# A gated cross-attention and mixture-of-experts block on one core: TensorE's order inside a step of the attention loop

## The reference

```python
h   = layernorm(x)                                  # x: 32 x 64 x 512, 2048 rows in all
q   = rmsnorm(h @ Wq.T  -> 32 heads x 128) * q_norm_w
k   = rmsnorm(ctx @ Wk.T -> 8 heads x 128) * k_norm_w
v   = ctx @ Wv.T                                    # 8 heads x 128, each serves 4 query heads
p   = softmax(q @ k.T / sqrt(128) + mask)           # 64 x 64 for each of 32 batches and 32 heads
x   = x + tanh(g_xattn) * ((p @ v) @ Wo.T)
h2  = layernorm(x)
out = x + tanh(g_ffn) * (shared_ffn(h2) + top-2-of-16 mixture of experts (h2))
```

## Time and profile before

| what | value |
|---|---|
| time, median of 3 executions | 1516.77 us (1516.59 to 1519.57) |
| time of the profiled execution | 1513.25 us |
| its span | 1511.2 us |
| TensorE matmuls busy | 1435.7 us, 95% of the span |
| VectorE busy | 852.8 us, 56% |
| ScalarE busy | 508.4 us, 34% |
| GpSimd busy | 353.0 us, 23% |
| chain that ended last | 90% of it on TensorE |

### The profile page before, as it was taken

One profiled execution on the slowest core, in us unless ns is written; L12 is line 12 of the kernel. 1 busy time (PEld: TensorE's weight loads), 2 busy tenths in 40 slices (PEclk: granted clock), 3 DMA queues, 4 the chain that ended last, 5 costly groups with the idle time before them and its releaser, 6 DMA issues.

```text
span 1511.2 us, 31305 instructions
## 1 busy us (share of the span) xinstructions
PE 1435.7 (95%) x10606; PEld 1222.2 (81%) x10607; DVE 852.8 (56%) x1839; ACT 508.4 (34%) x1130; POOL 353.0 (23%) x407
## 2 busy tenths in 40 slices
PE   6999999999999999999999999999997999999980
PEld 5888888888888888888888888888885888777760
DVE  5444446656566566665665666656879532233335
ACT  4333343333333333333333333333334411222210
POOL 1222232211212212112122121221212071233335
PEclk9999999999999999999999999999998999999995
DMA  6534331111111111111111111111224083355548
GB/s 217 160 118 132 121 112 39 35 39 32 42 35 35 38 38 35 38 31 42 35 35 38 36 37 39 32 38 54 69 69 154 21 177 103 130 165 165 167 156 261
DMA packets 92737, 125.39 MB, mean 83 GB/s; under 512 B 9009, under 2 KB 58208, under 8 KB 92192
## 3 DMA queue, kind: packets, MB, share of 16 engines
q1 hardware_dynamic: 85360, 104.21, 22.3%
q0 software_dynamic: 7344, 20.73, 4.8%
HBM read 87.39 MB, written 37.53 MB: 83 GB/s over the span
## 4 chain that ended last, share of the span: by engine, by line
PE 90%; DMA 3%; DVE 3%; issue 1%; POOL 1%; ACT 0%; SPq 0%; POOLq 0%; DVEq 0%
PE ps L499 23%; PE ps L501 22%; PE ps L500 22%; PE ps L774 5%; PE ps L566 5%; PE ps L606 4%; PE ps L790 3%; PE ps L575 2%; PE ps L592 2%; DMA y<-ybuf,sli 1%; PE ps L769 1%; POOL y L479 1%; DMA acc<-in_wv 1%; PE ps L547 1%; DMA wgu<-in_w_gu 1%
## 5 line engine op out<-in xcount | busy, mean ns | idle before, releaser
L422 POOL TENSOR_TENSOR qr<-qv,mhalf 128x8 f32<-128x8 f32 x64 | 105.1, 1642 | 733.8 <-DVE qv L1123 733.8
L499 PE MATMUL ps<-hT,w0h 128*128 (+2 forms) x640 | 199.1, 311 | 0.9 <-DVE w0l L1056 0.9
L501 PE MATMUL ps<-hT,w0h 128*128 (+2 forms) x640 | 196.2, 306 | 0.0
L500 PE MATMUL ps<-hT,w0l 128*128 (+2 forms) x640 | 196.0, 306 | 0.0
L1108 DVE TENSOR_TENSOR acc<-ps,acc 128x512 f32 (+1 forms) x129 | 88.7, 688 | 146.6 <-PE ps L501 146.6
L932 ACT CAST ah<-ps 128x256 fp32r<-128x256 f32 x256 | 83.5, 384 | 256.7 <-PE ps L501 253.9
L1114 DVE TENSOR_TENSOR al<-ps,ah 128x256 fp32r<-128x256 f32 x256 | 96.2, 418 | 99.4 <-ACT ah L932 99.2
L499 PE MATMUL ps<-hT,w1h 128*128 (+1 forms) x512 | 147.6, 288 | 0.0
L500 PE MATMUL ps<-hT,w1l 128*128 (+1 forms) x512 | 145.1, 283 | 0.0
L501 PE MATMUL ps<-hT,w1h 128*128 (+1 forms) x512 | 145.0, 283 | 0.0
L499 PEld LDWEIGHTS ps<-hT,w0h 128*128 128x128 f32 x640 | 123.2, 192 | 7.8 <-DVE w0l L1056 1.1
(11 more groups left out here) (211 smaller groups left out, 3179.1 us busy)
## 6 DMA issues: line engine op xcount, KB each, us to landing
wraw<-in_w_att SPq DMA_DIRECT2D x64, 256.0 KB, 2.6
ybuf<-ye SPq DMA_DIRECT2D x47, 256.0 KB, 2.0
vbuf<-vo SPq DMA_DIRECT2D x16, 512.0 KB, 3.3
kbuf<-ko SPq DMA_DIRECT2D x16, 512.0 KB, 3.8
kt<-kbuf SPq DMA_DIRECT2D x64, 128.0 KB, 2.0
vt<-vbuf SPq DMA_DIRECT2D x64, 128.0 KB, 2.0
wgu<-in_w_gu SPq DMA_DIRECT2D x4, 2048.0 KB, 12.8
craw<-in_ctxT SPq DMA_DIRECT2D x9, 512.0 KB, 4.9
```

What stands on the lines that cost most here:

```text
L422: pool.tensor_tensor(qr[:], qv[:], mhalf[:, 0:8], ALU.pow).then_inc(q_rt, 1)
L499: pe.matmul(dst, l_hi, r_lo, start=first, stop=False)
L500: pe.matmul(dst, l_lo, r_hi, start=False, stop=False)
L501: return pe.matmul(dst, l_hi, r_hi, start=False, stop=last)
```

## The change

TensorE's order in a step becomes Q 1 to 4, transposes, scores, sums, both output projections of step i - 1, and then probabilities times v. The transposed probabilities go to PS[0] instead of PS[2] and PS[3]. TensorE waits ahead of them until ScalarE has squared the new Q there. The scores wait for the two copies of Q one by one. ScalarE's and VectorE's queues are reordered to match: ScalarE splits its weight slice and makes the exponentials ahead of `a_hi_tile`, and VectorE runs `a_rest` at the end of its step. Before the loop, GpSimd clears all of `ah` and `al` instead of half of each. As both projections lag by a step, step 0 projects two cleared tiles instead of one, and four tiles instead of three are projected behind the loop: tiles 0 and 1 of step 62 around the last transposes, tiles 0 and 1 of step 63 at the end. The diff, with little context:

```diff
@@ -415,7 +415,7 @@
             for t in (ah, al):
-                pool.memset(t[:, 1].rearrange("p h b s -> p (h b s)").bitcast(F32), 0.0).then_inc(acc_zero, 1)
+                pool.memset(t[:].rearrange("p a h b s -> p (a h b s)").bitcast(F32), 0.0).then_inc(acc_zero, 1)
@@ -558,9 +558,9 @@
             def scores(j):
-                pe.wait_ge(q_copy, 2 * j + 2)
                 pe.wait_ge(kt_in, 16 * j + 16)
                 for hp in range(2):
+                    pe.wait_ge(q_copy, 2 * j + 1 + hp)
                     for b in range(CB):
@@ -589,7 +589,8 @@
                     src = pb[:, CB * (m // 2) + 2 * (m % 2):CB * (m // 2) + 2 * (m % 2) + 2, :]
-                    mm = pe.transpose(PS[2 + m % 2][:, m // 2 * P:(m // 2 + 1) * P], src.rearrange("p b s -> p (b s)"), ident[:])
+                    c0 = m % 2 * HG * S + m // 2 * P
+                    mm = pe.transpose(PS[0][:, c0:c0 + P], src.rearrange("p b s -> p (b s)"), ident[:])
                 mm.then_inc(pT_done, 1)
@@ -608,7 +609,13 @@
-            def step(i, chunk_q, w_q, w_o, w_before, q_ready, o_ready):
+            def project_tile(i, bp, w_o):
+                pe.wait_ge(a_hi, 4 * i + 6 + 2 * bp)
+                pe.wait_ge(a_lo, 4 * i + 6 + 2 * bp)
+                pe.wait_ge(acc_done, 2 * i + 3 + bp)
+                project_out(bp, w_o, (0, 1, 2, 3))
+
+            def step(i, chunk_q, w_q, w_o, q_ready, o_ready):
@@ -618,18 +625,15 @@
                 q_head(1, 0, chunk_q, w_q)
+                q_head(1, 1, chunk_q, w_q).then_inc(q_done, 1)
+                pe.wait_ge(q_sq, 2 * i + 3)
                 transpose_probs(i)
-                q_head(1, 1, chunk_q, w_q).then_inc(q_done, 1)
-                probs_v(i)
                 scores(i + 1)
                 q_sums(i + 1)
-                pe.wait_ge(acc_done, 2 * i + 1)
-                project_out(1, w_before, (0, 1, 2, 3))
                 pe.wait_ge(w_lo, o_ready)
-                pe.wait_ge(a_hi, 4 * i + 6)
-                pe.wait_ge(a_lo, 4 * i + 6)
-                pe.wait_ge(acc_done, 2 * i + 2)
-                project_out(0, w_o, (0, 1, 2, 3))
+                for bp in range(2):
+                    project_tile(i - 1, bp, w_o)
+                probs_v(i)
@@ -639,11 +643,11 @@
             def group(i0, p, last=False):
-                step(i0, 1, W[p], W[p], W[1 - p], None, i0 + 8)
+                step(i0, 1, W[p], W[1 - p], None, i0 + 8)
                 with pe.Fori(0, NC - 2) as t:
-                    step(i0 + 1 + t, t + 2, W[p], W[p], W[p], None, i0 + 8)
+                    step(i0 + 1 + t, t + 2, W[p], W[p], None, i0 + 8)
                 if not last:
-                    step(i0 + NC - 1, 0, W[1 - p], W[p], W[p], i0 + 12, i0 + 8)
+                    step(i0 + NC - 1, 0, W[1 - p], W[p], i0 + 12, i0 + 8)
@@ -651,20 +655,12 @@
-            pe.wait_ge(acc_done, 2 * STEPS - 1)
-            pe.wait_ge(a_hi, 4 * STEPS)
-            pe.wait_ge(a_lo, 4 * STEPS)
-            project_out(1, W[1], (0, 1, 2, 3))
+            project_tile(STEPS - 2, 0, W[1])
             transpose_probs(STEPS - 1)
+            project_tile(STEPS - 2, 1, W[1])
             probs_v(STEPS - 1)
-            pe.wait_ge(a_hi, 4 * STEPS + 2)
-            pe.wait_ge(a_lo, 4 * STEPS + 2)
-            pe.wait_ge(acc_done, 2 * STEPS)
-            project_out(0, W[1], (0, 1, 2, 3))
-            pe.wait_ge(a_hi, 4 * STEPS + 4)
-            pe.wait_ge(a_lo, 4 * STEPS + 4)
-            pe.wait_ge(acc_done, 2 * STEPS + 1)
-            project_out(1, W[1], (0, 1, 2, 3))
+            project_tile(STEPS - 1, 0, W[1])
+            project_tile(STEPS - 1, 1, W[1])
@@ -686,7 +682,7 @@
                 if c == 2:
-                    pe.wait_ge(acc_done, 2 * STEPS + 3)
+                    pe.wait_ge(acc_done, 2 * STEPS + 4)
                 for k in range(KD):
@@ -921,12 +917,10 @@
                 for bp in range(2):
-                    act.copy(pt[0][:, bp, :], PS[2 + bp][:, 0:HG * S]).then_inc(pT_hi, 1)
+                    act.copy(pt[0][:, bp, :], PS[0][:, bp * HG * S:(bp + 1) * HG * S]).then_inc(pT_hi, 1)
...
             def a_hi_tile(i, bp):
-                if bp == 1:
-                    act.wait_ge(o_done, 2 * i + 1)
-                    act.wait_ge(a_lo, 4 * i + 6)
+                act.wait_ge(o_done, 2 * i + 1 + bp)
                 for b2 in range(2):
@@ -940,13 +934,13 @@
                 squares(0, i + 1)
-                probs_hi(i)
                 q_out(1, i + 1)
                 squares(1, i + 1)
+                probs_hi(i)
+                split_slice(i, w, sl)
+                exps(i + 1)
                 a_hi_tile(i, 0)
                 a_hi_tile(i, 1)
-                split_slice(i, w, sl)
-                exps(i + 1)
@@ -1110,7 +1104,7 @@
                 for b2 in range(2):
-                    dve.wait_ge(a_hi, 4 * i + 5 + 2 * bp + b2)
+                    dve.wait_ge(a_hi, 4 * i + 7 + b2)
                     dve.tensor_tensor(al[:, bp, :, b2, :], pv_view(bp, b2), ah[:, bp, :, b2, :],
@@ -1148,9 +1142,9 @@
             def probs_lo(i):
+                dve.wait_ge(pT_hi, 2 * i + 2)
                 for bp in range(2):
-                    dve.wait_ge(pT_hi, 2 * i + 1 + bp)
-                    dve.tensor_tensor(pt[1][:, bp, :], PS[2 + bp][:, 0:HG * S], pt[0][:, bp, :],
+                    dve.tensor_tensor(pt[1][:, bp, :], PS[0][:, bp * HG * S:(bp + 1) * HG * S], pt[0][:, bp, :],
                                       ALU.subtract).then_inc(pT_evac, 1)
@@ -1168,21 +1162,17 @@
-            def dve_step(i, w, sl, tile, tile_before, complete=(None, None)):
-
-                probs_lo(i)
-                if complete[0] is not None:
-                    residual(complete[0], 1)
+            def dve_step(i, w, sl, tile, complete=None):
+
+                softmax(i + 1, lambda: probs_lo(i), lambda: add_out(2 * i + 1, 0, tile))
+                slice_lo(i, w, sl)
+                add_out(2 * i + 2, 1, tile + 1)
                 a_rest(i, 0)
-                if complete[1] is not None:
-                    residual(complete[1], 0)
-
-                def while_root():
-                    add_out(2 * i + 1, 1, tile_before)
-                    a_rest(i, 1)
-
-                softmax(i + 1, while_root, lambda: add_out(2 * i + 2, 0, tile))
-                slice_lo(i, w, sl)
+                a_rest(i, 1)
+                if complete is not None:
+                    dve.wait_ge(acc_done, 2 * i + 4)
+                    for q in range(2):
+                        residual(complete + q, q)
@@ -1192,10 +1182,9 @@
             def group(i0, p):
-                dve_step(i0, W[1 - p], 0, 0, NT - 1)
-                with dve.Fori(0, NC - 2) as t:
-                    dve_step(i0 + 1 + t, W[1 - p], t + 1, 2 * t + 2, 2 * t + 1)
-                dve_step(i0 + NC - 1, W[1 - p], NC - 1, NT - 2, NT - 3)
+                dve_step(i0, W[1 - p], 0, NT - 2)
+                with dve.Fori(0, NC - 1) as t:
+                    dve_step(i0 + 1 + t, W[1 - p], t + 1, 2 * t)
@@ -1207,11 +1196,10 @@
             i0 = STEPS - NC
-            dve_step(i0, W[0], 0, 0, NT - 1)
+            dve_step(i0, W[0], 0, NT - 2)
             dve.wait_ge(const_act, 1)
-            dve_step(i0 + 1, W[0], 1, 2, 1, (None, 0))
-            with dve.Fori(0, NC - 3) as t:
-                dve_step(i0 + 2 + t, W[0], t + 2, 2 * t + 4, 2 * t + 3, (2 * t + 1, 2 * t + 2))
+            with dve.Fori(0, NC - 2) as t:
+                dve_step(i0 + 1 + t, W[0], t + 1, 2 * t, 2 * t)
@@ -1245,30 +1233,33 @@
             i = STEPS - 1
-            add_out(2 * i + 1, 1, 13)
+            statistics(0)
+            add_out(2 * i + 1, 0, 12)
             probs_lo(i)
-            statistics(0)
+            for n in range(2):
+                normalise(n)
+            dve.wait_ge(acc_done, 2 * i + 3)
+            residual(12, 0)
+            add_out(2 * i + 2, 1, 13)
             a_rest(i, 0)
             a_rest(i, 1)
-            residual(11, 1)
-            residual(12, 0)
-            for n in range(4):
+            for n in range(2, 4):
                 normalise(n)
             shift(0)
-            dve.wait_ge(acc_done, 2 * i + 3)
+            dve.wait_ge(acc_done, 2 * i + 4)
             residual(13, 1)
...
             slice_lo(i, W[0], NC - 1)
-            add_out(2 * i + 2, 0, 14)
-            dve.wait_ge(acc_done, 2 * i + 4)
+            add_out(2 * i + 3, 0, 14)
+            dve.wait_ge(acc_done, 2 * i + 5)
             residual(14, 0)
-            add_out(2 * i + 3, 1, 15)
             shift(1)
+            add_out(2 * i + 4, 1, 15)
             for n in range(4):
...
                     normalise(n + 4)
-            dve.wait_ge(acc_done, 2 * i + 5)
+            dve.wait_ge(acc_done, 2 * i + 6)
             residual(15, 1)
```

## The result

| | median | lowest to highest | executions |
|---|---|---|---|
| kernel before | 1516.68 us | 1515.22 to 1519.57 | 4 |
| changed kernel | 1531.88 us | 1530.76 to 1533.58 | 4 |

The ratio is 1.0099, with a 95% interval of [1.0081, 1.0116]: slower by 1%, 15.2 us where +9.8 was forecast. The profiled execution of the changed kernel took 1531.7 us, with a span of 1530.0.

What follows compares the result with a forecast made beforehand. TensorE was taken to bound the kernel, at 14.43 us a step without a long wait. Loop +9.3, head -3.3 and behind the loop +3.8 made +9.8 us, 1526.6 against the median 1516.77; range 1517 to 1534.

Steps and rivals of the forecast that it cites:

- Shape changes in the step: Five changes of array shape per step instead of four: +0.15 us a step, ends 0.00 and +0.22, over 62 steps +9.3.
- Into v: New border from projection to probabilities times v: 0.09 at the start and 0.10 in the first distance, 0.19 us a step.
- v to Q: New border from probabilities times v to the next Q: 0.18 us a step, below 0.08, above 0.22.
- transposes to scores: New border from the transposes to the scores: 0 to 0.10 us a step, taken as 0.07.
- covers of 0.26 and 0.30: Spare us in a step for the second copy of Q ahead of the scores, and the squares ahead of the sums.
- rival (c): A new wait in the step, for Q's second copy or the squares: 0.2 to 0.4 us more, 1539 to 1552, chance 0.09.
- The relieved wait: TensorE's transposes waiting for the probabilities: claimed to cost nothing in the 62 steps, so moving them relieves nothing.
- The head: Step 0: the fourth Q fills idle time ahead of the probabilities, about 2.4 us idle remain; taken as -3.3 us.
- Behind the loop: After the loop, one more tile and one more v to do, plus longer waits: +3.8 us, ends +2.6 and +4.8.
- The forecast's second wait of 3.3: Behind the loop, TensorE ahead of step 63's projection, held by VectorE's two normalisations, a residual and an addition: 3.3 us.
- The first wait, 3.6: Behind the loop, TensorE ahead of step 62's projection of tile 0, waiting for `a_rest` in VectorE's queue: about 3.6 us.
- SP's transfers: Waits for the next weights and for v: each has a step's length, costed at nothing.

## Why the prediction was right, and where its sizes were off

Direction and mechanism held; 1531.88 lies in the range, above the 1526.6 by 5.3.

- **Shape changes in the step: right, mis-sized by 0.08.** Forecast +0.15 a step, measured +0.23 (14.66 for 14.43), so 62 x 0.08 = 5 us. Into v 0.19 as forecast, v to Q 0.19 for 0.18, transposes to scores 0.10 for 0.07. Removed were 0.19 + 0.10 = 0.29, put at 0.30. These terms give 0.48 - 0.29 = +0.19. Of the rest, 0.03 is in the projections' block, 5.71 where 5.59 + 0.09 were to be expected, and 0.01 is the lower pace at the start. The 0.03 lies in the matmuls right behind the sums' border, and why they are slower is open. That the step goes by the number of shape changes is shown by the kernels with 15.11 (two more) and 14.44 (one less), which have the transposes and their bank where the changed kernel has them. The kinds of border count too: out of or into the 64 rows of v 0.19 from or to the full array, the others 0.10 or 0.11 in these rows; the one from scores to sums can't be separated in the merged rows, and it stands in both orders. The 0.23 is a little over the forecast's upper end of 0.22 a step.
- **The rule beside the rows.** The rows show a first start late by about 0.09 and a first distance late by about 0.10 at changes between the full array and 64 rows. The Trainium skill, TensorEngine Tiling (Array Packing), section Tiling Modes, has a drain at each change of mode: by that rule two more changes must cost. The trace of the kernel with v in two parts agrees, with 0.46 us a step for two. The page gives no duration.
- **No wait in the step: right.** The covers of 0.26 and 0.30 held. The kernel with one wait for Q is rival (c) made real, +0.35 a step.
- **The relieved wait: right.** The old order's transposes stood behind Q without a gap; kernels with the transposes behind all four Q, and four shape changes, have the same 14.44 step as before. Their new place gives nothing.
- **The head: right.** TensorE waits 2.46 us in step 0 (forecast 2.4), and the head is 3.59 shorter (3.3), in an execution in which the pace fell behind that wait, as the forecast assumed. Where it doesn't fall, the gain is larger by up to 1.5. The forecast could not know which of the two it would be; its middle value was one of them.
- **Behind the loop: right in kind, mis-sized, and the step that failed is an addition.** +8.9 for +3.8. The forecast has TensorE end its projections "about 4 us later": 2.7 for a tile, 0.9 for a v, "and 0.4 as the difference of the waits". But its own waits are 3.6 and 3.3 where there were 0.84 and 1.24, a difference of 4.8, or 3.6 with the wait of 1.19 that it left out. Measured, the waits are 8.60 for 3.27, so +5.33, and TensorE comes to the row behind its projections (line 677, now 673) 31.47 us behind the first projection of step 62 (1174.34) instead of 21.56 (1152.42): 9.9 later. That is 3.6 of work, 5.3 of waits and about 1.0 of lower pace. VectorE's row at 1156.05, put 2.6 later, is 7.5 later by the same count (at 1175.60). The 4.9 that are missing in "0.4" are nearly the whole 5.1 by which this part was short.
- **A term put at nothing, inside it.** "SP's transfers ... I cost all these at nothing" was argued for the transfers within a step, and the loads of x behind the loop hang on the last transposes, which the change delays by a projection. VectorE's queue then waited 3.32 us for a residual with the splits behind it. The forecast's second wait of 3.3 came out at 4.89, and at 1.90 with the load early, so the queue of VectorE that it had counted was not what held TensorE. The first wait, 3.6 for 3.71, was right.
- **The sum.** Loop +5.2, behind the loop +5.1, head -0.3 and untouched parts -1.0 make the 9.0 us by which the span's difference of 18.8 exceeds the forecast. That the median misses by 5.3 only, and stays in the range, is partly luck. The forecast added the 3.5 us by which before's profiled execution lay under its median; that of the changed kernel lay 0.2 under, which takes 3.3 off, and the time outside the span was 1.7 us for 2.05, which takes another 0.35.

## What to carry to other kernels

In an order of matmuls that leaves TensorE no idle time, count the changes of array shape per step before counting waits: here one cost 0.1 us, or 0.2 between the full array and 64 rows, and an order that was to save a wait which was already covered lost by adding a change. When two waits are forecast, add them up against all the old ones in the same stretch, from the whole timeline: the larger error here was in that sum, not in the waits. When an instruction moves later, follow each queue that waits for it to the end of the kernel, SP's too: a load that is early enough in the loop can be the last thing to arrive behind it. And when an engine's row is many times its usual length, look at the row that runs beside it.

## What the hardware showed unexpectedly

- **GpSimd beside VectorE.** VectorE's `tensor_scalar` of 128x512 took 4.43 us instead of 0.54 beside GpSimd's `tensor_tensor` of 4.51, and ended 0.28 behind it. The Trainium skill, SBUF — State Buffer, section Who interferes with whom, has it that the two engines share one pair of ports, that certain VectorE operations take it whole, and that the one that comes second is blocked to the end of the other. The trace agrees. In a step of the changed kernel the product at line 1142 runs beside GpSimd's split of v, which has moved there, and takes 1.49 us for the two halves instead of 0.76. It ends at 609.37, 4.0 us ahead of the transposes that need it, so this costs nothing. Its timeline:

```profile
607.88 1.49 DVE L1142 TENSOR_TENSOR pb<-pb,rc 128x256 f32<-128x256 f32 x2
608.30 0.80 POOL L430 TENSOR_TENSOR vtl<-vt,vth 128x256 fp32r<-128x256 f32 x1
```

- **Weight loads at a change of shape.** With one shape, the load of the next weights starts a matmul ahead (606.11 for 606.33). At the changes into v, into Q, into the scores and into the projection it starts with the first matmul of the new shape (606.64, 607.55, 613.93 and 615.59 for matmuls at 606.65, 607.55, 613.94 and 615.59). That is where the 0.1 us stand.
- **The clock behind a wait.** After 4.89 us idle TensorE's granted clock was 0.50, the 1.2 GHz level, for the next 4.0 us (1166.80 to 1170.80), and matmuls of 512 columns stood 0.43 apart instead of 0.23. After 3.71 us it was 0.50 in all of the next 5.26 us in one execution, and 0.61 in the mean of 4.43 us in another, with the same matmuls. After 2.46 us in step 0 it fell in one execution and not in another, see above. So a wait can cost more than its own length, and not always the same.
